# A four-stage graph network on one core: mask sums ahead of put-off products, and the second layer's adjacency product taken chunk by chunk

## The reference

```python
x = layernorm(x + L0(x, adj))   # signed attention, 3 heads, two gated (GRU) cells
x = layernorm(x + L1(x, adj))   # neighbour mean:  h = x @ neigh_W.T
                                #   h = adj @ h / (adj.sum(1) + 1)
                                #   z = concat([x, h]) @ lin_W.T
x = layernorm(x + L2(x, adj))   # attention over non-zero entries, exp(leaky_relu(el_i + er_j))
x = layernorm(x + L3(x, adj))   # relu(adj @ x @ W + b), layernorm, state-space scan
```

## Time and profile before

| | |
|---|---|
| runs | 960.3 median of 3 (959.52 to 1486.46) |
| profiled execution, its own time | 959.17 |
| its span | 957.4 |
| mean granted TensorE clock | 0.945 of full speed |
| TensorE busy | 858.2 (90%) |
| VectorE busy | 698.1 (73%) |
| ScalarE busy | 504.3 (53%) |

### The profile page before, as it was taken

How to read it: one execution, slowest core, us unless ns; L and a number is a source line. 1 busy time by engine, 2 the same in 40 slices (tenths; PEclk the granted TensorE clock), 3 DMA queues, 4 the chain that set the end, 5 groups by cost and what they waited for, 6 DMA issues and landing times. The chain is left out here.

```text
span 957.4 us, 11888 instructions
## 1 busy us (share of the span) xinstructions
PE 858.2 (90%) x4199; PEld 557.3 (58%) x4199; DVE 698.1 (73%) x1026; ACT 504.3 (53%) x763; POOL 233.0 (24%) x128
## 2 busy tenths in 40 slices
PE   6999969999999999997899899979599799798765
PEld 6665528888888888843454589934234344342322
DVE  3986979999999998157800549671486887889996
ACT  2754446877777777445010256305375675676541
POOL 2000000000000000000210010000687777778981
PEclk8999999999999999999799769999799999999978
DMA  7689875122022201096100000000422222123120
GB/s 272 234 299 352 303 279 209 75 88 88 0 88 88 88 0 44 23 425 257 26 1 0 1 1 1 1 23 3 170 75 99 76 80 103 73 80 121 55 66 12
DMA packets 37825, 102.41 MB, mean 107 GB/s; under 512 B 4587, under 2 KB 9597, under 8 KB 31253
## 3 DMA queue, kind: packets, MB, share of 16 engines
q1 hardware_dynamic: 37220, 101.58, 29.1%
q10 hardware_dynamic: 560, 0.27, 0.1%
HBM read 83.70 MB, written 18.14 MB: 106 GB/s over the span
## 5 line engine op out<-in xcount | busy, mean ns | idle before, releaser
L1584 PE MATMUL PS<-big 128*128 128x256 f32 x768 | 193.9, 384 | 4.4 <-ACT big L1413 4.2
L207 PE MATMUL PS<-ident,big 128*128 128x128 f32 x1123 | 159.1, 282 | 21.8 <-DVE big L1783 7.8
L207 PEld LDWEIGHTS PS<-ident,big 128*128 128x128 f32 x1123 | 138.0, 146 | 43.5 <-issue 22.9
L374 POOL TENSOR_TENSOR big<-big 128x1024 f32<-128x1024 f32 x64 | 149.2, 2351 | 15.0 <-DMA big<-b_dram 7.8
L1584 PEld LDWEIGHTS PS<-big 128*128 128x128 f32 x768 | 133.4, 190 | 22.6 <-ACT big L1413 8.0
L861 PE MATMUL PS<-big,ident 128*128 128x512 f32 x256 | 128.7, 644 | 17.1 <-DVE big L1158 17.1
L1413 ACT ACTIVATE big<-PS 128x512 f32<-128x512 f32 x192 | 105.0, 599 | 57.8 <-PE PS L207 56.9
L1147 DVE TENSOR_TENSOR_SCAN big<-PS,stripes,big 128x512 f32<-128x512 f32 x96 | 117.1, 1266 | 8.1 <-ACT PS L572 7.8
L572 ACT ACTIVATE PS<-big,stripes 128x512 f32<-128x512 f32 x128 | 85.7, 685 | 61.7 <-DVE big L1147 61.5
L333 POOL MEMSET big<- 128x16 f32 x1 | 0.1, 126 | 465.2 <-DVE big L965 465.2
L1783 DVE SCALAR_TENSOR_TENSOR big<-big,rz 128x2048 f32<-128x2048 f32 x48 | 112.7, 2350 | 0.9
(11 more groups left out here) (196 smaller groups left out, 985.7 us busy)
## 6 DMA issues: line engine op xcount, KB each, us to landing
big<-in_adj SPq DMA_DIRECT2D x16, 2048.0 KB, 9.1
big<-at_dram SPq DMA_DIRECT2D x4, 4096.0 KB, 27.2
big<-b_dram SPq DMA_DIRECT2D x16, 1024.0 KB, 4.8
at_dram<-big SPq DMA_DIRECT2D x3, 4096.0 KB, 16.8
big<-b_dram SPq DMA_DIRECT2D x23, 256.0 KB, 5.2
at_dram<-big SPq DMA_DIRECT2D x1, 3072.0 KB, 18.2
big<-e_dram SPq DMA_DIRECT2D x3, 1024.0 KB, 6.8
big<-e_dram SPq DMA_DIRECT2D x2, 768.0 KB, 5.2
```

Of the source, the lines that this page charges most:

```text
L207: return nc.tensor.transpose(PS[:, bank, col:col + P], src, ident[:])
L374: nc.gpsimd.tensor_tensor(dbu[k % 3], du[c % 2], bb[group % 2][:, k % 4, :].unsqueeze(1).to_broadcast([P, DI, CH]), ALU.mult).then_inc(dbu ...
L1584: m = nc.tensor.matmul(PS[:, 4 + k // 3, 0:256], hw[:, jt, h, :], qt[v % 4][:, 256 * c:256 * c + 256], start=(h == 0 and jt == 0), stop=(h ...
```

## The change

Two places change, and with them the root of two norms.

1. At the end of stage 1 the mask sums of tile 15 come straight after those of tile 14. `node_support` of the last chunk is put behind them: tile 0 before the small products, tiles 1 to 15 after.
2. `adjacency_product` takes a chunk c and a range of row tiles. Chunk 0 is done first with all 16 row tiles, then chunks 1, 2 and 3. While a chunk runs, the product with lin_W of the chunk before (`neighbours`), the transposes (`next_features`) and the scores (`next_scores`) of the chunk two before stand in between. ScalarE's list is interleaved to match, and `norm` scales a quarter at once for k = 1.
3. For k = 1 and 2, ScalarE computes exp(-0.5 ln(v)) in two instructions instead of a square root, and VectorE's reciprocal goes. One preload of the tables for exp and ln stands ahead of the second layer's copies.

```diff
@@ -176,7 +176,7 @@
         l2_v, l2_vec, l2_x, l2_xev = sem("l2_v"), sem("l2_vec"), sem("l2_x"), sem("l2_xev")
-        gru_step = sem("gru_step")
+        gru_step, x_log = sem("gru_step"), sem("x_log")
         ones_ready, walb_ready, x_plus_b = sem("ones_ready"), sem("walb_ready"), sem("x_plus_b")
@@ -400,8 +400,13 @@
                 act.wait_ge(var_ready, 4 * k + q + 1)
-                nc.scalar.activation(rstd[:, 4 * q:4 * q + 4], mv[:, 4 * q:4 * q + 4, 1], ACT.Sqrt,
-                                     bias=cst[:, 0:1]).then_inc(std_ready, 1)
+                cols = slice(4 * q, 4 * q + 4)
+                if k == 0:
+                    nc.scalar.activation(rstd[:, cols], mv[:, cols, 1], ACT.Sqrt, bias=cst[:, 0:1]).then_inc(std_ready, 1)
+                else:
+                    nc.scalar.activation(rstd[:, cols], mv[:, cols, 1], ACT.Ln, bias=cst[:, 0:1]).then_inc(x_log, 1)
+                    act.wait_ge(x_log, 4 * (k - 1) + q + 1)
+                    nc.scalar.activation(rstd[:, cols], rstd[:, cols], ACT.Exp, scale=-0.5).then_inc(std_ready, 1)
@@ -434,8 +439,7 @@
                 evac(l1_h, q + 1, H1, q, 4 + q, l1_hev)
-            for q in range(4):
-                evac(l1_mm, q + 1, AHT, q, q, l1_aev)
+            nc.scalar.preload_act_table_set("natural_log_exp_and_others")
@@ -443,14 +447,15 @@
-            root(1, 0)
-            for q in range(3):
-                xt_copy(2, q, q)
-                root(1, q + 1)
-            right_factor(0)
+            for q in range(4):
+                evac(l1_mm, q + 1, AHT, q, q, l1_aev)
+                if q < 3:
+                    root(1, q)
+                if q:
+                    xt_copy(2, q - 1, q - 1)
+                    right_factor(q - 1)
+            root(1, 3)
             xt_copy(2, 3, 3)
-            right_factor(1)
-            right_factor(2)
             right_factor(3)
@@ -652,15 +657,15 @@
-            def adjacency_product(weights, q, done):
-
-                pe.wait_ge(diag_back, q + 1)
-                for jt in range(4 * q, 4 * q + 4):
-                    for c in range(NCH):
-                        m = nc.tensor.matmul(PS[:, c, :], weights[:, jt, :], AT[:, jt, c * CH:(c + 1) * CH],
-                                             start=(jt == 0), stop=(jt == NT - 1))
-                        if jt == NT - 1:
-                            m.then_inc(done, 1)
+            def adjacency_product(weights, c, first, last, done):
+
+                for jt in range(first, last):
+                    if c == 0 and jt % 4 == 0:
+                        pe.wait_ge(diag_back, jt // 4 + 1)
+                    m = nc.tensor.matmul(PS[:, c, :], weights[:, jt, :], AT[:, jt, c * CH:(c + 1) * CH],
+                                         start=(jt == 0), stop=(jt == NT - 1))
+                if last == NT:
+                    m.then_inc(done, 1)
@@ -708,27 +713,28 @@
             pe.wait_ge(l1_hev, 1)
-            adjacency_product(hj, 0, l1_mm)
+            adjacency_product(hj, 0, 0, 4, l1_mm)
             for q in range(1, 4):
...
             pe.wait_ge(l1_hev, 4)
-            adjacency_product(hj, 1, l1_mm)
+            adjacency_product(hj, 0, 4, NT, l1_mm)
             for q in range(4):
                 tiles_product(q, 4 + q, XT, wt[:, 13, :], l1_a)
-            adjacency_product(hj, 2, l1_mm)
-            adjacency_product(hj, 3, l1_mm)
-            for q in range(4):
+
+            def neighbours(q):
+
                 pe.wait_ge(l1_aev, q + 1)
...
-            pe.wait_ge(w2_in, 16)
-            pe.wait_ge(walb_ready, 1)
-            pe.wait_ge(l1_add, 4)
-            for q in range(4):
+            def next_features(q):
+
                 pe.wait_ge(x_ready, 4 + q + 1)
                 xt_fill(2, q, q, X)
+
+            def next_scores(q):
+
                 pe.wait_ge(xt_ev, 8 + q + 1)
@@ -737,6 +743,26 @@
                     m.then_inc(l2_v, 1)
+
+            for c in range(1, NCH):
+                adjacency_product(hj, c, 0, 4, l1_mm)
+                neighbours(c - 1)
+                adjacency_product(hj, c, 4, 8, l1_mm)
+                if c == 2:
+                    pe.wait_ge(w2_in, 16)
+                    pe.wait_ge(walb_ready, 1)
+                    pe.wait_ge(l1_add, 4)
+                if c >= 2:
+                    next_features(c - 2)
+                adjacency_product(hj, c, 8, 12, l1_mm)
+                if c >= 2:
+                    next_scores(c - 2)
+                adjacency_product(hj, c, 12, NT, l1_mm)
+            next_features(2)
+            neighbours(3)
+            next_scores(2)
+            next_features(3)
+            next_scores(3)
@@ -960,17 +986,19 @@
                     dve.wait_ge(std_ready, 4 * k + q + 1)
-                    link(nc.vector.reciprocal(rstd[:, 4 * q:4 * q + 4], rstd[:, 4 * q:4 * q + 4]))
+                    if k == 0:
+                        link(nc.vector.reciprocal(rstd[:, 4 * q:4 * q + 4], rstd[:, 4 * q:4 * q + 4]))
                     for i in range(4 * q, 4 * q + 4):
...
+                at_once = k == 1
                 for q in range(4):
-                    if q == 1:
+                    if q == 1 and not at_once:
                         scale(0)
                     residual(q)
-                    if q > 1:
+                    if q > 1 and not at_once:
                         scale(q - 1)
@@ -978,7 +1006,10 @@
                     m.then_inc(var_ready, 1)
-                scale(3)
+                    if at_once:
+                        scale(q)
+                if not at_once:
+                    scale(3)
@@ -1552,13 +1583,12 @@
                     rest_of_setup()
-            node_support(NCH - 1, 0, 4)
             sign_sums(NT - 1)
-            node_support(NCH - 1, 4, 5)
+            node_support(NCH - 1, 0, 1)
             pe.wait_ge(es_last, 1)
...
             attention_rows(NCH - 1)
-            node_support(NCH - 1, 5, NT)
+            node_support(NCH - 1, 1, NT)
...
             pe.sem_inc(tr2, 24)
```

## The result

The changed kernel took 945.86 us in the median of four runs (943.92 to 949.58), the kernel before 959.91 in four (957.58 to 1486.46; the disturbed run of 1486.46 is left out of the ratio, and without it the median is 959.52). Ratio 0.9873, 95% interval 0.9845 to 0.9901: faster by 1.3%, less than the 2% that count as a change, and outside the forecast range of 949 to 957.5. Six more runs of the same kernel, beside 17 of the one before (959.01), gave a median of 949.71 and 0.989 (0.9867 to 0.9912), just inside the range. All ten runs of it lie between 943.92 and 950.29.

The account below looks back on a forecast made before the run. TensorE, busy 90% of the span, bounds the kernel, with a mostly latency-bound 26.3 us tail in the second layer. Gains 1.8 + 5.2 + 0.2 = 7.2 take 959.17 to 952.0, plus 1.1 gives 953.1; range 949 to 957.5.

Parts of the forecast that it names:

- Part 4: Second layer's tail: only chunk 3's chain left, third layer starts 11.7 us after the product ends, at the lower clock.
- part 3: Second layer's product: lin_W products, transposes and scores put into it lengthen it by 7.8 us, none of it waiting.
- the 0.7 for changes of kind: Second layer's product: seven excursions to other work cost TensorE 0.1 us each at the changes, 0.7 in all.
- Part 1: End of stage 1: earlier mask sums let VectorE open the attention sooner, gain 1.8 us, bounds 1.6 and 3.6.
- The count of some 17.7 waiting records: End of stage 1: TensorE's sequencer signals with about 17.7 records still waiting, so VectorE waits until about 127.05.
- the queue of 64 instructions: End of stage 1, rival: all 30 records fit TensorE's queue, signal isn't late, another 1.8 us, 951.3; chance 0.10.
- Part 2: Start of the second layer: TensorE waits 1.6 us for the last transposes, chunk 0 ends later, loss 1.6 us.
- the tail is shorter: Rival, second layer's tail: clock stays high into the third layer, 1.6 us less for scores, some more behind, 951; chance 0.10.
- Part 5: Roots of the norms as exp and ln, with table loads moved: gain 0.2 us, between -1.3 and 0.8.
- the slower ones: Rivals in the second layer: short clock dip (956, chance 0.13), lasting dip (963.4, 0.05), chunk order feeding nobody (958.5, 0.04).
- no wait inside chunks 1 to 3: Sign in the second layer's product: a wait above 0.3 us there would make the inserted-work estimate wrong.
- the dip: Rival, start of second layer: TensorE's waits lower the granted clock for a few us, +3, 956; chance 0.13.

Follow-up runs that it names:

- e1: Kernel before with only the mask sums of tile 15 moved ahead of the put-off product: 957.96 against 958.22, ratio 0.9985.
- e3: Changed kernel with the semaphore additions to tr2 and qt_used moved ahead of the last 15 products of node_support: 948.09 against 958.22 before, ratio 0.9896.
- e4: Kernel before with only the roots as exp(-0.5 ln) and the table preload, TensorE's orders unchanged: 957.26 against 958.22, ratio 0.997.
- g3: Changed kernel with five idle products filling TensorE's gaps in the second layer's tail: 949.47, ratio 0.989 to the kernel before.
- g1: Changed kernel run again, unaltered: 949.71 against 959.01 for the kernel before, ratio 0.989.
- e2: Changed kernel with the end of stage 1 (mask sums) put back as before: 950.91 against 958.22 for the kernel before, ratio 0.9928.
- h1: Changed kernel with GpSimd's bias addition held back until eight of the third layer's sixteen weight tiles are ready: 948.78 against 958.54 before, ratio 0.99.
- g4: Changed kernel with idle filler products in the tail and the signal to VectorE ahead of the last 15 put-off products: 947.22 against 959.01 before, ratio 0.9879.
- h2: Changed kernel with early signal, tail fillers, and GpSimd's addition held back to the eighth weight tile: 946.56 against 958.54 before, ratio 0.9888.
- h4: Changed kernel with early signal, tail fillers, and GpSimd's addition held back until all sixteen weight tiles are ready: 943.29 against 957.95 before, ratio 0.9845.

## Why the prediction was wrong

The forecast was 953.1 with a sum of 7.2; the spans differ by 13.1 in the first profile and by 9.5 in the repeat, the medians by 14.1 (13.7 without the disturbed run) and 9.3. The first median lies outside the range, the repeat's inside, so part of the miss is the scatter of single runs.

The step that failed is where the sum ends. Part 4 stops at VectorE's first operation of the third layer, and but for the roots everything behind it was put at nothing. Two terms stand there in the first profile, both of the granted clock: the third layer's 33rd record came 1.76 earlier still (9.98 for 11.74), and the last products of the kernel 2.74 earlier (14.69 for 17.43). Together they are 4.5 of the 5.85 by which the span fell further than the 7.2. The product and the tail gave another 0.9, of which 0.75 is one term of part 3, the 0.7 for changes of kind, which measured 0; the roots gave 0.2 more, and 0.2 lie elsewhere. The 1.76 is there again in the repeat (1.67); the 2.74 isn't, so that part of the miss is chance and not the change's.

- **Part 1, 1.8: right.** 1.74 in three profiles (e1, changed, repeat). The count of some 17.7 waiting records decided it: the signal was late as forecast, and e3 shows that it was the limit. By the queue of 64 instructions that the Trainium skill gives (TensorE: Matmul & The Clock Gate, section Architectural detail) the flag would have set the start; it didn't.
- **Part 2, a loss of 1.6: right in its point, not in its price.** From the `memset`, the product goes on after 348.29; the forecast has 477.2 - 128.86 = 348.3. The wait of 1.6 is there in the repeat (1.66) and filled by slow records in the first. The kernel before doesn't always reach the point as early as in its profile: from the `memset` to the last record it took 401.49 there, 402.56 in e1 and 402.22 in e4, while all kernels with the new order and work in between took 410.1 to 410.4. So against e1 and e4 the loss is 0.7 to 1.1 smaller. In these traces a slower TensorE there costs nothing, because VectorE sets the pace.
- **Part 3, 7.8: too much by 0.75.** The term that was off: "Seven excursions cost a little at each change of kind ... I take 0.1: 0.7". They cost nothing. A set of eight narrow records adds 0.89, of transposes 0.44, of scores 1.75 (1.67, and 0.08 in the record behind it): 3 x 0.89 + 2 x 0.44 + 2 x 1.75 = 7.05. The stretches agree: the product took 73.51 - 65.95 = 7.56 longer, and 0.5 of that is the loss of part 2 inside it (11.70 from its first record to 475.24, for 6.25 + 1.31 + 3.61 = 11.17 without a wait).
- **Part 4, a tail of 11.7: right.** 11.6 (537.5 to 549.06), at the lower clock, as assumed. g3 gives the bound at the full one, 1.65 less.
- **Behind the tail: missing, 1.7.** The clock was back for the first 32 records, which it was not before. I had this inside the rival *the tail is shorter*, as "some more behind", and gave it 0.10. It isn't sure either. With the same tail, the 33rd record came 9.98, 10.07 and 10.25 behind VectorE's first operation in three profiles (changed, g1, e3), and 13.19 and 11.67 in two (e2, and h1 with GpSimd's addition moved), in which the lower clock lasted into these records; the mean of the five is 11.0, 0.7 under the kernel before. What makes it last longer in some executions no run shows.
- **Part 5, 0.2: small in any case.** 0.44 in the third norm, and e4 shows it with the roots alone.
- **The rest of the first profile**, 2.74 in the last products and 0.1 to 0.2 elsewhere, isn't the change's: the repeat has -0.03 there.

In both profiles of the changed kernel stand 1.74 + (14.72 - 8.61) + 1.7 + 0.4 = 10.0, where 14.72 is the shorter tail (26.73 - 12.01) and 8.61 the longer way from the `memset` to the product's last record (410.10 - 401.49). That is 1.0% of 959, about what the second comparison measured (1.1%), and 2.8 over the forecast. Of these, 1.7 is the clock behind the tail, 0.9 the product and tail, 0.2 the roots. The other four microseconds of the first result are gone in the repeat; 2.74 of them are seen, in where the low clock fell in the profiled run, the rest I can't place, since the other runs left no trace. Single runs of one kernel are spread over 10 us (the kernel before: 953.99 to 963.76 in 23), and the range made no room for that.

Of the rivals, none of the slower ones came: the granted clock stayed at 1.00 from the product's rise (469.7, in the repeat 467.4) to the tail (544.8 and 545.9), across the repeat's wait of 1.66, and there is no wait inside chunks 1 to 3. The row by which the prediction argued against the dip, 631 to 637 us, is weaker than it reads: the clock had been low just ahead of it, from 627.0 to 630.4, 1.2 us after a wait of 3.07 for VectorE.

## What to carry to other kernels

Cut the span at marks that both kernels have, and follow a gain past the place where the change ends: what lies behind a shorter tail can start at another clock or beside another engine's work. Before a wait is priced, find out which engine sets the point where it ends; here a slower TensorE ahead of a point that VectorE sets cost nothing. The range of a forecast needs a term for the spread of one kernel's own runs, here 5 us either way for a single run.

## What the hardware showed that I had not expected

- A `sem_inc` of TensorE behind a run of products was issued when 17 records were still waiting (some 17.7 by time), with 22 records in the run and with 30, and in the changed kernel it was 2.0 us late for that (e3). Given ahead of products that the waiting engine doesn't need, it cost nothing in e3, g4, h2 and h4.
- One VectorE `tensor_scalar` over 128x2048 took 1.35, 1.72, 2.29 (e2) or 3.39 us, by how much of it lay beside a GpSimd addition of 4.52; it ended 1.08 or 1.09 behind the addition in the last three. A `scalar_tensor_tensor` pair went from 4.49 to 8.71 beside it, and the addition itself from 4.52 to 5.48.
- Changes of kind between wide products, narrow products and transposes cost TensorE nothing that the starts show (0.90, 0.44 and 1.67 for the sets put in, the sum of their records).
- Two executions of the same program had their last products at the full clock and mostly at the lower one, 2.77 us apart (14.69 and 17.46 from the last scan to the end).
